# First layer's deformable sampling: tent arrays stored point by point, x tents and weight table in PSUM, table rows copied one by one for GpSimd

## Chip, cores and metric

One Trainium2 chip, one core. The metric is the device time of one execution in microseconds (us), median of the runs; each profile is of one execution. PE is TensorE, DVE VectorE, ACT ScalarE, POOL GpSimd, SP SyncE.

## What is computed

Two layers, each a sampling convolution and a mixture of experts, on x of shape (4, 16, 16, 64). Only the first layer's convolution is touched. Per position it has 8 groups of 8 channels and 9 sampling points with an offset (x and y) and a softmax mask:

```python
xp = x @ in_w + in_b
x1 = silu(batchnorm(depthwise3x3(x)))
offset = x1 @ off_w + off_b                       # 8 groups * 9 points * 2
mask = softmax((x1 @ mask_w + mask_b).reshape(N, H, W, 8, 9), -1)
# each point: bilinear sample of xp (zero outside) at its own place + offset
out = (samples * mask).sum(-1) @ out_w + out_b
x = x + out
```

A bilinear sample is a sum over image positions with weights max(0, 1 - |dx|) * max(0, 1 - |dy|), the product of two "tents".

## The kernel before

1024 positions lie as 128 partitions x J = 8 positions. The kernel is written engine by engine; each engine's instructions run in the order written, and semaphores join them. For offsets below 2 in size a point reaches 5 x 5 displacements around its own place (D0 = 5), and with the 3 x 3 points all lie in a window of N0 x N0 = 7 x 7 displacements; the four corners are left out, and so are those of the 5 x 5. If an offset is larger, a flag sends the program through a general loop, which does not run here.

**Tents.** `ox`, `oy` (offsets) and `ml` (mask logits) have 576 = 8 positions x 8 groups x 9 points columns, the point innermost. ACT makes tents as `Abs` (L618) and `Relu(1 - a)` (L620), in the order x tent 0, y tents 2 to 4, x tents 1 to 4. DVE makes y tents 0 and 1 (L1118 to L1121) and multiplies the other y tents by the mask's exponentials (L1127). Before that it adds biases (L1105), takes the maximum over the points (L1111) and subtracts it (L1112).

**Table.** 21 products of an x tent and a y tent (`tent_product`, L291) of 576 columns are summed into a table of 7 x 7 displacements x 64 columns, in `big` from `AW`. `A_OWNER` shares them out: POOL 10 and DVE 3 go through `ring` to PE, which adds them into banks 0 to 6 of PSUM by 3 matmuls with the identity (L757, 192 columns read with a step of 9); DVE keeps 8 and adds them to the table in SBUF (L1147). When a row of the table (one x displacement) is complete, DVE joins the bank to the SBUF part (`join`, L1139), 7 times. POOL first sets the table to zero (L451).

**Products.** For each of 45 displacements the slab of the image (`big`, loaded by SP's DMAs L365 into 7 shifted slabs, semaphore `slab0`) is multiplied by its table column, spread over 8 channels (`slab_product`, L298, 512 columns). `PATTERN` gives POOL 25, DVE 6 for PE, and DVE 14 that it sums itself (L1217). PE sums the other 31 in bank 7 (L770). Between these DVE computes the flag (L1190 to L1199, PE transposes it at L775, DVE ends it at L1065 and L1066 and loads it to a register), then the sums of the exponentials and their reciprocals (L1224, L1225). L1228 adds the two sums, L1290 multiplies by the reciprocals, and everything after waits for that.

In the second layer's sampling L269 is the like product (POOL from SBUF; DVE with weights in PSUM), L1487 DVE's sum with the running sum in PSUM, L277 makes those weights (two inputs in SBUF), L909 is PE's sum, L927 a matmul of 144 columns.

Of the kernel before, what the change touches and what calls it, by code (L numbers as in the profile page):

```python
# [30 lines left out]
ALU = mybir.AluOpType  # L31
# [4 lines left out]
P = 128  # L36
# [37 lines left out]
def program(nc, a, out):  # L74
    ctx = ExitStack()
    with ctx:
# [152 lines left out]
        TX, TY = N0 * SLAB0, N0 * SLAB0 + D0 * J * GP0  # L229
        AW = TY + D0 * J * GP0  # L230
        A_PITCH = N0 * J * G0
        NA = N0 * A_PITCH
        assert AW + NA <= BIG
# [61 lines left out]
        def slab_product(eng, w, slot):  # L295

            wx, wy = divmod(w, N0)
            return eng.tensor_tensor(V(ring, 0, slot, [[1, P], [C0, J * G0], [1, C0]]),  # L298
                                     bigv(wy * SLAB0 + wx * C, [C0, J * G0], [1, C0]),
                                     bigv(AW + wx * A_PITCH + wy * J * G0, [1, J * G0], [0, C0]), ALU.mult)  # L300

# [114 lines left out]
        def _(pool):  # L416
# [34 lines left out]
            gp.memset(bigv(AW, [1, NA]), 0.0).then_inc(sem("A_zero"), 1)  # L451

            i = 0
            for dx in range(D0):
                for dy in range(D0):
                    if A_OWNER(dx, dy) == "pool":
                        pool.wait_ge(sem("tenty"), dy + 1)
                        pool.wait_ge(sem("tentx"), dx + 1)
                        if i >= 3:  # L460
                            pool.wait_ge(sem("a_ps"), A_COUNT("pool", i - 3))
                        tent_product(gp, dx, dy, POOL0 + J * GP0 * (i % 3)).then_inc(sem("a_pool"), 1)
                        i += 1

            pool.wait_ge(sem("slab0"), 128)
            pool.wait_ge(sem("a_ps"), A_TOTAL)
            order = [w for w in DISPLACED if OWNER(w) == "pool"]
            for i, w in enumerate(order):
                pool.wait_ge(sem("A_done"), w // N0 + 1)
                if i >= 4:  # L470
                    pool.wait_ge(sem("acc0"), PE_COUNT(order[i - 4]))
                slab_product(gp, w, POOL0 + 512 * (i % 4)).then_inc(sem("pool_pr0"), 1)
# [107 lines left out]
        def _(act):  # L580
# [27 lines left out]
            made = {"tentx": 0, "tenty_raw": 0}  # L608
            for n, (name, src, base, k) in enumerate(
                    [("tentx", ox, TX, 0)] + [("tenty_raw", oy, TY, k) for k in range(DVE_TENTS, D0)] +  # L610
                    [("tentx", ox, TX, k) for k in range(1, D0)]):
                if n == 1:
                    act.wait_ge(sem("mask_in"), 1)
                    sc.activation(ml[:, :], ml[:, :], ACT.Exp).then_inc(sem("mask_e"), 1)
                    act.wait_ge(sem("offy"), 1)
                if n:
                    act.wait_ge(sem(before), made[before])
                sc.activation(abx[:, :], src[:, :], ACT.Abs, bias=cval[:, k:k + 1]).then_inc(sem("abx"), 1)  # L618
                act.wait_ge(sem("abx"), n + 1)
                sc.activation(bigv(base + k * J * GP0, [1, J * GP0]), abx[:, :], ACT.Relu, bias=1.0,  # L620
                              scale=-1.0).then_inc(sem(name), 1)
                made[name] += 1
                before = name

            act.wait_ge(sem(before), made[before])
            sc.activation(abx[:, :], ox[:, :], ACT.Abs).then_inc(sem("off_abs"), 1)
            act.wait_ge(sem("tenty"), DVE_TENTS)
# [66 lines left out]
        def _(pe):  # L694
# [56 lines left out]
            for n, (dx, dy) in enumerate(A_ORDER):  # L751
                who = A_OWNER(dx, dy)
                i = A_ORDER_OF(who).index((dx, dy))
                pe.wait_ge(sem("a_pool" if who == "pool" else "a_dve"), i + 1)
                slot = POOL0 + J * GP0 * (i % 3) if who == "pool" else J * GP0 * (i % 2)
# [6 lines left out]
            seen = {"pool": 0, "dve": 0}  # L762
            first = True
            for w in PE_ORDER:
                who = OWNER(w)
                i = seen[who]
                seen[who] += 1
                pe.wait_ge(sem("pool_pr0" if who == "pool" else "dve_pr0"), i + 1)
                slot = (POOL0 if who == "pool" else 0) + 512 * (i % 4)
                mm(bank(7, 0, P, [1, 512]), ident[:, :], ring[:, slot:slot + 512], start=first,  # L770
                   stop=(w == PE_ORDER[-1])).then_inc(sem("acc0"), 1)
                first = False
                if w == PE_ORDER[FLAG_AT[1]]:
# [1030 lines left out]
```

## Time and profile before

| | |
|---|---|
| median of 3 runs | 337.71 us (337.0 to 338.55) |
| profiled execution, its own time | 335.97 us |
| its span, first to last instruction | 334.2 us |
| mean granted clock of TensorE | 0.856 of full speed |
| busy share PE, DVE, ACT, POOL | 69%, 67%, 17%, 50% |
| DMA | 10.84 MB |

### The profile page before, as it was taken

Reading aid. Unit: us, or ns where it says so; the run is one execution under the profiler, and the core shown is the slowest. Engines: PE = TensorE matmul, PEld = TensorE weight load, DVE = VectorE, ACT = ScalarE, POOL = GpSimd, SP = SyncE. Lnnn points to the kernel's source line nnn. Section 1 sums busy time; section 2 is a strip of 40 time slices with the busy share of each in tenths; the row PEclk is TensorE's granted clock in tenths of the full one; section 3 lists DMA queues with packets and bytes.
Section 4 is the critical chain, followed back from the end, with each engine's and each line's share of the span. In section 5 each row is a group of like instructions: output and inputs, shape, how many; then the busy total and the mean of one; then the engine's idle time right before and its main releaser. Section 6 shows DMA issues by size and latency. Waiting matters only on the chain.

```text
span 334.2 us, 2821 instructions
## 1 busy us (share of the span) xinstructions
PE 230.9 (69%) x864; PEld 133.2 (40%) x864; DVE 223.2 (67%) x469; ACT 55.4 (17%) x91; POOL 168.7 (50%) x198
## 2 busy tenths in 40 slices
PE   1939595987948496998898477589689884038600
PEld 0715464632313264322353133257367744017500
DVE  7768999979998865747330876998995245502207
ACT  1306910000000014542401100011001203003100
POOL 5700762379849832681100599799975020530071
PEclk9989696978969959799999697999979996558955
DMA  4477920000000000000019100000000000010101
GB/s 150 134 148 153 204 48 0 0 0 1 0 0 1 1 2 0 1 0 3 0 31 206 30 3 0 1 0 0 3 0 0 2 0 0 17 55 0 41 20 43
DMA packets 8237, 10.84 MB, mean 32 GB/s; under 512 B 4571, under 2 KB 5083, under 8 KB 8155
## 3 DMA queue, kind: packets, MB, share of 16 engines
q1 hardware_dynamic: 7708, 10.12, 13.1%
q0 software_dynamic: 512, 0.53, 0.6%
q8 instruction: 7, 0.11, 0.1%
q14 instruction: 10, 0.08, 0.1%
HBM read 8.03 MB, written 2.61 MB: 32 GB/s over the span
## 4 chain that ended last, share of the span: by engine, by line
DVE 31%; PE 29%; issue 17%; POOL 8%; ACT 2%; DMA 1%; DVEq 0%; POOLq 0%; ACTq 0%
DVE ring L298 5%; PE ps L757 4%; PE ps L909 4%; DVE ps L1487 4%; DVE ring L1217 4%; POOL ring L269 3%; PE ps L884 3%; DVE ps L277 2%; POOL slots_in L568 2%; PE ps L935 2%; PE ps L797 2%; PE ps L720 2%; PE ps L819 2%; DVE ring L291 2%; PE ps L701 1%
## 5 line engine op out<-in xcount | busy, mean ns | idle before, releaser
L269 POOL TENSOR_TENSOR ring<-big 128x384 f32<-128x384 f32 x72 | 57.9, 842 | 5.0 <-DVE ps L1487 4.6
L909 PE MATMUL ps<-ring,ident 128*128 128x384 f32 x100 | 38.5, 528 | 12.5 <-POOL ring L269 6.3
L298 POOL TENSOR_TENSOR ring<-big 128x512 f32<-128x512 f32 x25 | 35.0, 1432 | 13.2 <-PE ps L770 6.7
L770 PE MATMUL ps<-ring,ident 128*128 128x512 f32 x62 | 33.6, 700 | 7.2 <-DVE ring L298 6.0
L701 PE MATMUL ps<-zero,ident 128*128 128x512 f32 x38 | 25.0, 813 | 16.8 <-DMA slots_in<-xn,idx_in 15.2
L757 PE MATMUL ps<-ring,ident 128*128 128x192 f32 x78 | 27.9, 529 | 7.8 <-DVE ring L291 4.3
L1487 DVE TENSOR_TENSOR ps<-ps,ring 128x384 f32<-128x384 f32 x46 | 25.8, 562 | 10.5 <-PE ps L909 8.4
L291 POOL TENSOR_TENSOR ring<-big 128x576 f32<-128x576 f32 x10 | 17.3, 1734 | 30.5 <-DVE big L1121 19.9
L909 PEld LDWEIGHTS ps<-ring,ident 128*128 128x128 f32 x100 | 18.9, 201 | 28.1 <-DVE ring L269 9.0
L438 POOL TENSOR_TENSOR rstd<-veps,mhalf 128x4 f32<-128x4 f32 x8 | 8.3, 1042 | 39.6 <-DVE veps L1044 39.5
L757 PEld LDWEIGHTS ps<-ring,ident 128*128 128x128 f32 x78 | 19.4, 253 | 16.4 <-DVE ring L291 5.5
L770 PEld LDWEIGHTS ps<-ring,ident 128*128 128x128 f32 x62 | 13.2, 222 | 26.9 <-issue 11.7
L298 DVE TENSOR_TENSOR ring<-big 128x512 f32<-128x512 f32 x20 | 22.5, 1154 | 1.2 <-DVE flagi L1066 1.0
L588 ACT COPY xT<-ps 64x512 f32<-64x512 f32 x8 | 4.5, 578 | 100.2 <-PE ps L709 100.2
L701 PEld LDWEIGHTS ps<-zero,ident 128*128 128x128 f32 x38 | 9.5, 267 | 27.1 <-DMA slots_in<-xn,idx_in 15.3
L269 DVE TENSOR_TENSOR ring<-big,ps 128x384 f32<-128x384 f32 x36 | 19.5, 546 | 0.1
L574 POOL DMA_INDIRECT big<-slots_out,idx_out x8 | 7.6, 952 | 23.5 <-DMA slots_out<-big 21.4
L1217 DVE TENSOR_TENSOR ring<-ring 128x512 f32<-128x512 f32 x13 | 15.1, 1165 | 0.1
L1369 DVE TENSOR_TENSOR big<-big,ps 128x512 f32<-128x512 f32 x16 | 10.3, 684 | 6.7 <-PE ps L805 6.7
L1147 DVE TENSOR_TENSOR big<-big,ring 128x576 f32<-128x576 f32 x8 | 14.3, 1790 | 0.2
L568 POOL DMA_INDIRECT slots_in<-xn,idx_in x8 | 8.0, 997 | 12.7 <-DVE idx_out L1544 10.6
L666 ACT COPY big<-ps 128x512 f32<-128x512 f32 x8 | 4.6, 586 | 58.4 <-PE ps L917 58.4
(269 smaller groups left out, 399.7 us busy)
## 6 DMA issues: line engine op xcount, KB each, us to landing
big<-pad SPq DMA_DIRECT2D x8, 392.0 KB, 9.0
big<-pad SPq DMA_DIRECT2D x8, 240.0 KB, 5.4
w<-in_w_dram SPq DMA_DIRECT2D x1, 520.0 KB
w<-in_w_dram SPq DMA_DIRECT2D x2, 256.0 KB
w<-in_w_dram SPq DMA_DIRECT2D x1, 512.0 KB
pad<-img SPq DMA_DIRECT2D x8, 64.0 KB, 2.0
pad<-zero SPq DMA_DIRECT2D x1, 484.0 KB, 3.7
pad<-zero SPq DMA_DIRECT2D x1, 400.0 KB, 4.3
```

Of the source, the lines that this page charges most:

```text
L269: return eng.tensor_tensor(V(ring, 0, slot * SP, [[1, P], [NJ * C, 3], [C1, NJ * G1], [1, C1]]), bigv((py + dy) * SLAB1 + (dx + j0) * C, [ ...
L291: return eng.tensor_tensor(ring[:, slot:slot + J * GP0], bigv(TY + dy * J * GP0, [1, J * GP0]), bigv(TX + dx * J * GP0, [1, J * GP0]), ALU ...
L298: return eng.tensor_tensor(V(ring, 0, slot, [[1, P], [C0, J * G0], [1, C0]]), bigv(wy * SLAB0 + wx * C, [C0, J * G0], [1, C0]), bigv(AW + ...
L568: gp.indirect_dma_start(out=slots_in.ap(), out_offset=bass.IndirectOffsetOnAxis(ap=idx_in[:, j:j + 1], axis=0), in_=xn[:, j, 0, :], in_off ...
L701: mm(bank(free_bank, 0, P, [1, 512]), ident[:, :], zero[:, 0:512], start=True, stop=True)
L757: last = mm(bank(px + dx, 0, P, [1, 3 * J * G0], off=dy * J * G0), ident[:, :], V(ring, 0, slot + 3 * px, [[1, P], [1, 3], [K, J * G0]]), ...
L770: mm(bank(7, 0, P, [1, 512]), ident[:, :], ring[:, slot:slot + 512], start=first, stop=(w == PE_ORDER[-1])).then_inc(sem("acc0"), 1)
L909: mm(bank(1 + i % 2, 0, P, [1, SP]), ident[:, :], ring[:, slot * SP:slot * SP + SP], start=(n == 0), stop=(n == len(srcs) - 1)).then_inc(s ...
L1147: v.tensor_tensor(dst, dst, V(ring, 0, SUM0 + J * GP0 * (i % 2), [[1, P], [3, 3], [1, 3], [K, J * G0]]), ALU.add).then_inc(sem("a_added"), 1)
L1217: v.tensor_tensor(acc, acc, V(ring, 0, OWN0 + 512 * ((i - 2) % 2), [[1, P], [1, 512]]), ALU.add).then_inc(sem("own_sum"), 1)
L1369: v.tensor_tensor(hid, hid, bank(6 + u % 2, 0, F0, [1, 512]), ALU.mult).then_inc(sem("hw"), 1)
L1487: v.tensor_tensor(acc, acc, ring[:, slot * SP:slot * SP + SP], ALU.add).then_inc(sem("s_add"), 1)
```

## The change

The three arrays hold the points outermost: column = point x 64 + position and group. The weights and biases are reordered outside to suit, and DVE's bias adds, maximum, subtraction and reduction get step 64. A tent product's three rows of points are then contiguous in `ring`, and PE reads them without a step.

Each x tent is written by ACT to PSUM bank 7 for its first 512 columns and to `big` (`TX8`) for the last 64; ACT waits with it until DVE has made all products of the x tent before. All 21 tent products are DVE's, as two instructions: 512 columns with the x tent from PSUM, 64 with both tents from SBUF (`A_SLOTS` = 3 slots). All are summed by PE; the table in SBUF, its zeroing, L1147 and the joins go. ACT copies rows 0 to 4 of the table to `big`, each as it is complete (`row_copied`); POOL has all 33 products of these rows (`POOL_W`), into 8 slots of its own in `big`. DVE has the 12 of rows 5 and 6 (`DVE_W`), with the table from PSUM. POOL's products are summed by DVE with the running sum in PSUM bank 0 (25 sums, `pool_sum`; 11 of them between the tent products of dx 2 to 4), except 7 that PE sums with DVE's 12.

```diff
         def tent_product(eng, dx, dy, slot):
-            return eng.tensor_tensor(ring[:, slot:slot + J * GP0],
-                                     bigv(TY + dy * J * GP0, [1, J * GP0]), bigv(TX + dx * J * GP0, [1, J * GP0]),
-                                     ALU.mult)
+            tent = TY + dy * J * GP0
+            eng.tensor_tensor(ring[:, slot:slot + 512], bigv(tent, [1, 512]), bank(7, 0, P, [1, 512]), ALU.mult
+                              ).then_inc(sem("a_dve"), 1)
+            eng.tensor_tensor(ring[:, slot + 512:slot + J * GP0], bigv(tent + 512, [1, J * G0]),
+                              bigv(TX8 + dx * J * G0, [1, J * G0]), ALU.mult).then_inc(sem("a_dve"), 1)
 ...
+            if w in POOL_W:
+                table = bigv(AW + wx * A_PITCH + wy * J * G0, [1, J * G0], [0, C0])
+            else:
+                table = bank(wx, 0, P, [1, J * G0], [0, C0], off=wy * J * G0)
 ...
 POOL:
-            gp.memset(bigv(AW, [1, NA]), 0.0).then_inc(sem("A_zero"), 1)
 ...
+            for i, w in enumerate(POOL_W):
+                pool.wait_ge(sem("row_copied"), w // N0 + 1)
+                if i >= PR_SLOTS:
+                    signal, count = POOL_FREED(i - PR_SLOTS)
+                    pool.wait_ge(sem(signal), count)
+                slab_product(gp, w, pool_slot(i, [C0, J * G0], [1, C0])).then_inc(sem("pool_pr0"), 1)
 ...
 ACT:
+            for k in range(1, D0):
+                distance(ox, k)
+                tent_x(k)
+                act.wait_ge(sem("tentx"), 2 * k + 2)
+                act.wait_ge(sem("a_ps"), A_BY(k - 1))
+                sc.copy(bigv(AW + (k - 1) * A_PITCH, [1, A_PITCH]), bank(k - 1, 0, P, [1, A_PITCH])
+                        ).then_inc(sem("row_copied"), 1)
 ...
 PE:
-                              V(ring, 0, slot + 3 * px, [[1, P], [1, 3], [K, J * G0]]), start=False,
+                              ring[:, slot + 3 * px * J * G0:slot + 3 * (px + 1) * J * G0], start=False,
 ...
+                if n == FLAG_AT[1]:
                     pe.wait_ge(sem("off_max"), 1)
+                    pe.wait_ge(sem("row_copied"), 3)
 ...
 DVE:
+            for q, (dx, dy) in enumerate(A_ORDER):
+                dve.wait_ge(sem("tentx"), 2 * dx + 2)
+                if q >= A_SLOTS:
+                    dve.wait_ge(sem("a_ps"), q - A_SLOTS + 1)
+                tent_product(v, dx, dy, J * GP0 * (q % A_SLOTS))
+                if dx >= 2 and dy >= 1:
+                    pool_sum()
 ...
+            for q, w in enumerate(DVE_W):
+                if q >= 4:
+                    dve.wait_ge(sem("acc0"), PE_SUMS.index(("dve", q - 4)) + 1)
+                slab_product(v, w, V(ring, 0, 512 * (q % 4), [[1, P], [C0, J * G0], [1, C0]])).then_inc(sem("dve_pr0"), 1)
 ...
+                pool_sum()
```

On DVE, in the table's second half, stood (L291 tent product, L1147 sum into the table, L1139 join):

```order
L291 TENSOR_TENSOR ring<-big 128x576 x2
L1139 TENSOR_TENSOR big<-big,ps 128x448
L1147 TENSOR_TENSOR big<-big,ring 128x3x192 x2
L291 TENSOR_TENSOR ring<-big 128x576 x2
L1139 TENSOR_TENSOR big<-big,ps 128x448
L1147 TENSOR_TENSOR big<-big,ring 128x3x192
L1139 TENSOR_TENSOR big<-big,ps 128x448 x3
```

Now it reads there (L293 and L295 are the two parts of a tent product, L1153 is the sum of a POOL product, `ps` its running sum or the x tent):

```order
L293 TENSOR_TENSOR ring<-big,ps 128x512
L295 TENSOR_TENSOR ring<-big 128x64
L1153 TENSOR_TENSOR ps<-big 128x512
L293 TENSOR_TENSOR ring<-big,ps 128x512
L295 TENSOR_TENSOR ring<-big 128x64
L1153 TENSOR_TENSOR ps<-ps,big 128x512
L293 TENSOR_TENSOR ring<-big,ps 128x512
```

Joins and sums into the table are gone from DVE, and sums of POOL's products, which stood behind the table, stand between the tent products.

On POOL, between the constants and the casts for the next stage, stood the table's zeroing, ten tent products and 25 slab products:

```order
L451 MEMSET big 128x3136
L291 TENSOR_TENSOR ring<-big 128x576 [waits tentx,tenty] x3
L291 TENSOR_TENSOR ring<-big 128x576 [waits a_ps,tentx,tenty] x7
L298 TENSOR_TENSOR ring<-big 128x512 [waits A_done,a_ps,slab0]
L298 TENSOR_TENSOR ring<-big 128x512 [waits A_done] x3
L298 TENSOR_TENSOR ring<-big 128x512 [waits acc0,A_done] x21
```

and now 33 slab products alone (L305):

```order
L305 TENSOR_TENSOR big<-big 128x512 [waits row_copied,slab0]
L305 TENSOR_TENSOR big<-big 128x512 [waits row_copied] x7
L305 TENSOR_TENSOR big<-big 128x512 [waits v_sum,row_copied] x14
L305 TENSOR_TENSOR big<-big 128x512 [waits acc0,row_copied]
L305 TENSOR_TENSOR big<-big 128x512 [waits v_sum,row_copied] x2
```

The wait for the whole table (`a_ps`) has given way to one for a row's copy, and from the ninth product on POOL waits for DVE's sums (`v_sum`) or PE's (`acc0`).

## Rows read from the trace of the kernel before

**Rows 1.** Windows: us, busy us of each engine, PEclk, DMA share, GB/s

```profile
36.80:70.60 33.80, 28.23 (x79) 19.55 (x80) 31.08 (x28) 6.36 (x10) 16.84 (x11) 0.80 0.22 42
70.60:115.50 44.90, 33.50 (x63) 13.01 (x61) 43.37 (x44) 0.00 (x0) 37.89 (x32) 0.85 0.00 0
```

**Rows 2.** Chain of waits from 66 to 116 us, shares by line

```profile
by line: DVE ring L298 32.0%; DVE ring L1217 25.2%; issue 18.4%; PE ps L770 7.6%; PE ps L757 6.2%; DVE big L1139 2.4%; DVEq L1203 1.6%; DVE ring L1228 1.4%; DVE m L1224 1.3%; DVE flagf L1197 1.3%; DVE r L1225 1.1%; DVE flagf L1198 0.5%; DVE
```

**Rows 3.** Timeline of DVE: start, us, instructions, idle before and releaser

```profile
68.91 1.68 DVE L1139 TENSOR_TENSOR big<-big,ps 128x448 f32<-128x448 f32 x3 [2.38 <-PE ps L757]
...
113.37 0.75 DVE L1224 TENSOR_REDUCE m<-ml 128x64 f32<-128x576 f32 x1
...
114.74 0.69 DVE L1228 TENSOR_TENSOR ring<-ring,ps 128x512 f32<-128x512 f32 x1
```

**Rows 4.** Instructions of line 298: ns min/median/max, first and last start

```profile
L298 POOL TENSOR_TENSOR ring<-big x25: 1069/1517/1585, 69.0 to 109.1; 128x512 f32<-128x512 f32 x25
L298 DVE TENSOR_TENSOR ring<-big x20: 679/1272/1558, 70.6 to 111.2; 128x512 f32<-128x512 f32 x20
```

**Rows 5.** Timeline, POOL alone, POOL beside DVE, DVE alone

```profile
69.01 2.11 POOL L298 TENSOR_TENSOR ring<-big 128x512 f32<-128x512 f32 x2 [6.50 <-issue]
...
71.07 11.88 POOL L298 TENSOR_TENSOR ring<-big 128x512 f32<-128x512 f32 x8
...
95.41 1.28 DVE L298 TENSOR_TENSOR ring<-big 128x512 f32<-128x512 f32 x2
```

**Rows 6.** Instructions of line 269, second layer

```profile
L269 POOL TENSOR_TENSOR ring<-big x72: 831/837/980, 192.7 to 254.6; 128x384 f32<-128x384 f32 x72
L269 DVE TENSOR_TENSOR ring<-big,ps x36: 543/546/555, 193.9 to 255.4; 128x384 f32<-128x384 f32 x36
```

**Rows 7.** Timeline of DVE and ACT before the first tent product

```profile
29.21 0.76 DVE L1112 TENSOR_TENSOR ml<-ml,m 128x576 f32<-128x576 f32 x1
...
30.93 0.68 ACT L614 ACTIVATE ml<-ml 128x576 f32<-128x576 f32 x1
...
34.58 3.34 DVE L1127 TENSOR_TENSOR big<-big,ml 128x576 f32<-128x576 f32 x3
...
35.35 0.68 ACT L620 ACTIVATE big<-abx 128x576 f32<-128x576 f32 x1
```

**Rows 8.** Instructions of line 1147

```profile
L1147 DVE TENSOR_TENSOR big<-big,ring x8: 1168/1974/2329, 41.8 to 65.3; 128x576 f32<-128x576 f32 x8
```

**Rows 9.** Timeline of PE, runs of passes

```profile
44.20 6.37 PE L757 MATMUL ps<-ring,ident 128*128 128x192 f32 x18
...
96.75 4.56 PE L770 MATMUL ps<-ring,ident 128*128 128x512 f32 x5 [0.83 <-DVE ring L298]
...
102.43 4.88 PE L770 MATMUL ps<-ring,ident 128*128 128x512 f32 x11
...
219.01 1.15 PE L927 MATMUL ps<-w_ua,big 128*128 128x144 f32 x8
```

**Rows 10.** Windows for clock and slabs; timeline of PE at its longest pause

```profile
42.00:43.00 1.00, 1.00 (x4) 0.90 (x4) 1.00 (x1) 0.97 (x3) 1.00 (x1) 0.50 1.04 201
43.00:44.00 1.00, 1.00 (x4) 0.69 (x4) 1.00 (x1) 0.42 (x1) 0.07 (x1) 0.96 0.83 156
...
95.54 0.37 PE L775 MATMUL ps<-ident,flagf 128*1 128x128 f32 x1 [3.41 <-DVE flagf L1199]
```

**Rows 11.** Timeline of POOL and DVE around the one-column instructions

```profile
92.92 2.55 POOL L298 TENSOR_TENSOR ring<-big 128x512 f32<-128x512 f32 x2
...
94.49 1.00 DVE L1199 SCALAR_TENSOR_TENSOR flagf<-flagf 128x1 f32<-128x1 f32 x1
```

**Rows 12.** Timeline of DVE after the flag's last step

```profile
104.09 1.19 DVE L298 TENSOR_TENSOR ring<-big 128x512 f32<-128x512 f32 x1 [0.95 <-DVE flagi L1066]
```

**Rows 13.** Instructions of line 277, and one of them in the timeline

```profile
L277 DVE TENSOR_TENSOR ps<-big x4: 641/1904/4409, 193.2 to 238.4; 128x216 f32<-128x216 f32 x4
...
208.45 3.05 DVE L277 TENSOR_TENSOR ps<-big 128x216 f32<-128x216 f32 x1
```

More of the change, by code:

```diff
@@ L607, in _ @@
             act.wait_ge(sem("cval"), 1)
[L608 to L617, printed above, removed]
-                sc.activation(abx[:, :], src[:, :], ACT.Abs, bias=cval[:, k:k + 1]).then_inc(sem("abx"), 1)
[L619 to L623, printed above, removed]
@@ L625, in _, with distance, tent_x @@
-            act.wait_ge(sem(before), made[before])
+            n_abs = 0
+            def distance(src, k):
+                nonlocal n_abs
+                sc.activation(abx[:, :], src[:, :], ACT.Abs, bias=cval[:, k:k + 1]).then_inc(sem("abx"), 1)
+                n_abs += 1
+                act.wait_ge(sem("abx"), n_abs)
+            def tent_x(k):
+                if k:
+                    act.wait_ge(sem("a_dve"), 2 * A_BY(k - 1))
+                sc.activation(bank(7, 0, P, [1, 512]), abx[:, 0:512], ACT.Relu, bias=1.0, scale=-1.0
+                              ).then_inc(sem("tentx"), 1)
+                sc.activation(bigv(TX8 + k * J * G0, [1, J * G0]), abx[:, 512:J * GP0], ACT.Relu, bias=1.0, scale=-1.0
+                              ).then_inc(sem("tentx"), 1)
@@ new lines, in _ @@
+            distance(ox, 0)
+            act.wait_ge(sem("offy"), 1)
+            tent_x(0)
+            act.wait_ge(sem("mask_in"), 1)
+            sc.activation(ml[:, :], ml[:, :], ACT.Exp).then_inc(sem("mask_e"), 1)
+            act.wait_ge(sem("tentx"), 2)
+            for k in range(DVE_TENTS, D0):
+                distance(oy, k)
+                sc.activation(bigv(TY + k * J * GP0, [1, J * GP0]), abx[:, :], ACT.Relu, bias=1.0, scale=-1.0
+                              ).then_inc(sem("tenty_raw"), 1)
+                act.wait_ge(sem("tenty_raw"), k - DVE_TENTS + 1)
@@ L627, in _ @@
+            for k in range(D0 - 1, POOL_ROWS):
+                sc.copy(bigv(AW + k * A_PITCH, [1, A_PITCH]), bank(k, 0, P, [1, A_PITCH])).then_inc(sem("row_copied"), 1)
             act.wait_ge(sem("tenty"), DVE_TENTS)
@@ L1172, in _ @@
-            for wx in range(D0 - 1, N0):
-                join(wx)
-            dve.wait_ge(sem("A_done"), N0)
-            dve.wait_ge(sem("slab0"), 128)
-            order = [w for w in DISPLACED if OWNER(w) == "dve"]
-            own = [w for w in DISPLACED if OWNER(w) == "sum"]
-            acc = V(ring, 0, SUM0, [[1, P], [1, 512]])
-            def product(w, slot):
-                return slab_product(v, w, slot)
-            todo = list(order)
-            k = 0
-            for i in range(len(own) + 1):
-                if i == FLAG_AT[0]:
+            acc = V(ring, 0, SUM0, [[1, P], [1, 512]])
@@ new lines, in _, with pool_sum @@
+            n_sum = 0
+            def pool_sum():
+                nonlocal n_sum
+                if n_sum == 0:
+                    dve.wait_ge(sem("row_copied"), 1)
+                else:
+                    dve.wait_ge(sem("v_sum"), n_sum)
+                i = DVE_SUMS[n_sum + 1]
+                dve.wait_ge(sem("pool_pr0"), i + 1)
+                first = pool_slot(DVE_SUMS[0], [1, 512]) if n_sum == 0 else bank(0, 0, P, [1, 512])
+                dst = bank(0, 0, P, [1, 512]) if n_sum < len(DVE_SUMS) - 2 else acc
+                v.tensor_tensor(dst, first, pool_slot(i, [1, 512]), ALU.add).then_inc(sem("v_sum"), 1)
+                n_sum += 1
```

201 lines of the change are left out of this document (65 added, 136 removed).

## The prediction

> **What bounds the kernel now.** I read the stages first. The first layer's sampling has two parts: the table of weights (36.8 to 70.6 us) and the 45 products with it (70.6 to 115.5). DVE is busy for 31.08 of 33.8 us and 43.37 of 44.9; PE and POOL have room [rows 1]. The chain of waits says the same of 66 to 116 us: DVE's products (L298) 32% and its sums (L1217) 25.2%, and only then PE [rows 2]. DVE stops twice for PE (2.38 us before the last joins, once for the flag), so a step taken off DVE moves the end. The end that counts is L1228, which adds DVE's sum to PE's: it starts at 114.74 and takes 0.69 us, so 115.4 [rows 3].
>
> **Why DVE is so slow there.** With both inputs in SBUF a DVE instruction and a POOL product stretch each other. L298 takes 679 ns at best and 1272 in the median on DVE, 1069 and 1517 on POOL [rows 4]. Eight POOL products beside such DVE work take 11.88 us, one each (11.88 - 1.52) / 7 = 1.48 us; two alone take 2.11, so 1.03 each [rows 5]. DVE alone issues one every 0.60 us (1.28 us for two [rows 5]), beside POOL every 1.48. With one input in PSUM it doesn't happen: in the second layer POOL's L269 has 831 to 980 ns while DVE's L269, with the weights in PSUM, stays at 543 to 555 [rows 6]. That is the change's lever: it puts x tents, table and sum in PSUM.
>
> **Start.** DVE's third L1127 waits for ACT's relu, which ends at 36.03, and the second was stretched by POOL's first tent product; three took 3.34 us [rows 7]. POOL's ten tent products go, so DVE starts tents at about 36.1 + 0.75 = 36.9 instead of 38.0. The strided edits (bias adds, L1111, L1112 and their new forms) cost nothing up to 0.95 us: the softmax shift ends at 29.97, the exponential waits for its table load until 30.93 [rows 7]. The strided max may go from 0.74 to 1.2 us (strided L1147 takes 1168 ns at least [rows 8], plain L1112 760 [rows 7]); that stays under the cover.
>
> **Table, tents of dx 0 and 1.** Eight tent products are now all DVE's, each 0.60 us plus a 64-column one. For the latter: 679 ns for 512 columns [rows 4] and 546 for 384 [rows 6] make 1.04 ns a column and 0.15 us fixed, so 0.21 for 64, less the 0.08 by which instructions overlap: 0.15 (bounds 0.07, its columns alone, and 0.30). 8 x 0.75 = 6.0. Bank 7 holds one x tent, so ACT may write the next only when DVE has read the last: a relu of 512 and one of 64 stand on the path, estimated from L620's 0.68 for 576 [rows 7] at 1.05 us with hand-overs (0.7 to 1.5). Twice: 2.1. The first eight end at 45.0. PE: its strided 192-column passes come every (6.37 - 0.52) / 17 = 0.344 us with the clock at full [rows 9]. Contiguous passes follow the columns: 0.429 us for 512 (11 take 4.88), 0.123 for 144, 0.85 for 512 at 1.2 GHz [rows 9]. So 192 cost 0.161 or 0.32, a tent's six passes 0.97 or 1.92 us instead of 2.06. The clock was at 0.50 at 42 us [rows 10], early in the table's build, before which PE has nothing to do; that pause stays, so with three slots PE holds DVE back by some 1.5 us. POOL's first product waits for the slabs, whose packets end at 43.8 [rows 10]; I take 44.8, when row 0 has long been copied.
>
> **Table, dx 2 to 4, beside POOL.** 13 tents, 11 of them followed by one sum of a POOL product. DVE's own pitch would be 0.60 + 0.15 + 0.60 = 1.35. But the 64-column product still has both inputs in SBUF. L1199, one column wide, took 1.00 us because POOL was in a product: both end at 95.5 [rows 11]. POOL's period is 1.03, so a round of 1.35 tends to last two periods, 2.06, except where POOL itself waits for a slot: I take 1.85. 11 x 1.85 + 2 x 1.0 + two hand-overs 2.1 = 24.5. The table ends at 45.0 + 1.5 + 24.5 = 71, no sooner than now. What is gained is that 19 products and 11 sums are done by then. The seven joins and eight L1147 (1168 to 2329 ns each) are gone [rows 8].
>
> **After the table.** 12 products and 14 sums at 0.60: 15.6 us. Flag: three reduces 0.75, the min (0.76, or 1.62 beside POOL), two tiny ones: 3.8; the sum of the exponentials and its reciprocal, 1.37 from 113.37 to 114.74, 1.7 in the strided form; the last flag step 1.4, of it 0.95 idle before the next product; waits and L1228 1.0 [rows 3, 12]. Together 23.5. PE has 19 sums of 0.86, 16 us, hidden at 2.4 GHz; at 1.2 they are 32 and bound. The three reduces leave PE without input for over 3 us; before, PE's 3.41 us pause for the flag [rows 10] was followed by passes of 0.85 us, the lower level [rows 9]. So I add 2.5 for PE. End: 71 + 23.5 + 2.5 = **97**, against 115.4: **18 us** less. POOL's 33 products need 33 x 1.03 = 34 us from 44.8; with eight slots they follow DVE's sums and end some 5 us before it. ACT's five copies of 448 columns, one instruction each like L620, hide under DVE; so do the waits added ahead of PE's flag transpose. The 334.2 - 115.5 = 218.7 us behind it are untouched. The profiled execution took 335.97 us (span 334.2); less 18 is 318. The median of the runs is 337.71, 1.7 above it, so **319.7 us** in such runs. A change of 0.5% (1.7 us) is about what can be told from none.
>
> **The port, row against rule.** L277 on DVE, 216 columns with both inputs in SBUF, took 641, 757 (by the median), 3051 and 4409 ns [rows 13]: at 0.8 us per L269 that is three and five POOL products of waiting in two of four. L298 on DVE never took more than 1558 ns, one POOL product and itself [rows 4]. The Trainium skill (SBUF — State Buffer, Who interferes with whom) says that whichever of the two starts first holds the shared port for its whole instruction and the other fully blocks until it finishes. By that each small product waits for at most one of POOL's, which gives the sum above; rows 11 agree, the long L277 don't, and they make the first rival.
>
> **Rivals.**
> 1. *POOL gets in again and again.* Each of the some 18 small products beside POOL waits one more product, some 0.6 to 1.0 us. POOL can't run on for long: it needs a slot that only DVE's sums free. The table ends 10 us later, the end is at 107: gain 8.5, 329 us. Two of four L277 speak for it, L298 against. Chance 0.22.
> 2. *POOL's slot waits leave the port free.* The rounds take 1.35 to 1.45: some 6 us less, end 91, gain 24.5: 313 us. Chance 0.07.
> 3. *PE stays at 1.2 GHz.* 63 x 2 x 0.32 = 40 us of table passes from 37.7, then 19 x 1.71 = 32, with gaps: 113. Gain 2.5, 335 us. Before, the clock was at 0.80 and 0.85 of full in these stages [rows 1]. Chance 0.05.
> 4. *Slower.* The same small product (L295 of the changed kernel), at the mean of the four L277, 2.2 us, in spite of the slots: 18 x (2.2 - 0.5) = 31 us more, end 128, 350 us. It turns slower where the mean wait is over 0.5 + 18 / 18 = 1.5 us. Chance 0.03.
>
> The forecast has 0.63. Range 312.5 to 329: case 1 is at its upper end and case 2 at its lower, cases 3 and 4 are left out. Faster by over 0.5%: 0.63 + 0.22 + 0.07 and half of case 3, 0.94; within 0.5% 0.03; slower 0.03.
>
> **What would show it.** Right: in the table stage the DVE product with a PSUM input stays at 0.68 us and POOL's at 1.07; the 64-column ones have a median between 0.3 and 0.9 us; the last table pass of PE ends near 71; POOL starts its first product at 44 to 45 and its last near 92; the final add is at 96 to 98. Wrong: 64-column products of 2 us and more, PE idle for ACT's relu by more than 1.5 us at each dx, PE passes of 192 columns that stay at 0.344, or a stage behind 97 us that is longer than 218.7.

## The result, and the profile after it

The changed kernel takes **315.35 us** (median of 4 runs, 315.16 to 315.57) against 337.36 (4 runs, 336.58 to 338.55): ratio 0.9345, 95% interval 0.9315 to 0.9375, 22.0 us less. The forecast was 319.7 with a range of 312.5 to 329. The profiled execution took 315.29 us, its span is 313.6, the mean clock 0.857. Between the two profiled executions the difference is 20.7 us (335.97 - 315.29): the kernel before was profiled in one of its faster executions.

Windows of the changed kernel (columns as in [rows 1]): from the first tents to the slabs' arrival, the rest of the table, the products behind it, and everything after.

```profile
33.50:44.00 10.50, 9.56 (x43) 9.56 (x44) 6.43 (x17) 2.80 (x7) 0.00 (x0) 0.70 1.03 202
44.00:70.50 26.50, 17.91 (x85) 14.49 (x83) 23.08 (x37) 5.08 (x10) 20.85 (x20) 0.94 0.00 1
70.50:94.60 24.10, 19.68 (x39) 7.27 (x39) 21.72 (x37) 1.12 (x2) 17.24 (x24) 0.93 0.01 2
94.60:313.60 219.00, 150.92 (x645) 88.38 (x645) 121.74 (x331) 35.22 (x64) 100.95 (x131) 0.83 0.07 17
```

The table ends where it did (70.5 against 70.6). But 20 of POOL's products lie in its second part, and the stage behind it takes 24.1 us instead of 44.9 [rows 1]. Behind it, 219.05 us against 218.8 (334.2 - 115.4) have not moved.

The instructions of the new lines (ns min/median/max, first and last start): L293 and L295 are the 512 and the 64 columns of a tent product, L305 a product with a table column, L1153 a sum of a POOL product.

```profile
L293 DVE TENSOR_TENSOR ring<-big,ps x21: 669/680/690, 33.6 to 67.8; 128x512 f32<-128x512 f32 x21
L295 DVE TENSOR_TENSOR ring<-big x21: 218/403/951, 34.2 to 68.4; 128x64 f32<-128x64 f32 x21
L305 POOL TENSOR_TENSOR big<-big x33: 1071/1077/1521, 45.5 to 88.8; 128x512 f32<-128x512 f32 x33
L305 DVE TENSOR_TENSOR ring<-big,ps x12: 677/678/687, 70.6 to 90.2; 128x512 f32<-128x512 f32 x12
L1153 DVE TENSOR_TENSOR ps<-ps,big x23: 685/693/700, 50.1 to 91.5; 128x512 f32<-128x512 f32 x23
L1153 DVE TENSOR_TENSOR ps<-big x1: 1482/1482/1482, 47.7 to 47.7; 128x512 f32<-128x512 f32 x1
```

What has one operand in PSUM stays within 3% of its median beside POOL. What has both in SBUF doesn't: 64 columns take 218 to 951 ns, and the one sum that starts from two SBUF inputs 1482 instead of 693. POOL's products are back from 1517 ns [rows 4] to 1077.

Timeline of the changed kernel, start of the sampling and the first rounds beside POOL (columns as in [rows 3]; L1098 is the first tap of the depthwise convolution, L752 the matmuls for offsets and mask):

```profile
12.46 0.52 DVE L1098 TENSOR_SCALAR cm<-cm,w_dc 128x572 f32<-128x572 f32 x1
...
21.14 3.20 PE L752 MATMUL ps<-w_om,o_tok 64*64 64x216 f32 x32 [3.25 <-ACT o_tok L596]
...
33.56 0.69 DVE L293 TENSOR_TENSOR ring<-big,ps 128x512 f32<-128x512 f32 x1
...
45.48 4.62 POOL L305 TENSOR_TENSOR big<-big 128x512 f32<-128x512 f32 x4 [33.22 <-DMA big<-pad]
...
47.70 1.48 DVE L1153 TENSOR_TENSOR ps<-big 128x512 f32<-128x512 f32 x1 [2.14 <-POOL big L305]
...
51.31 0.95 DVE L295 TENSOR_TENSOR ring<-big 128x64 f32<-128x64 f32 x1
52.18 0.69 DVE L1153 TENSOR_TENSOR ps<-ps,big 128x512 f32<-128x512 f32 x1
52.78 0.67 DVE L293 TENSOR_TENSOR ring<-big,ps 128x512 f32<-128x512 f32 x1
53.37 0.95 DVE L295 TENSOR_TENSOR ring<-big 128x64 f32<-128x64 f32 x1
```

The last rows are one round: from one L295 to the next 2.06 us, two of POOL's periods. Later POOL has to wait for a free slot in each round, and a round takes 1.91 us (POOL's product, the L295 that waits for it, and the next L295):

```profile
66.14 1.08 POOL L305 TENSOR_TENSOR big<-big 128x512 f32<-128x512 f32 x1 [0.83 <-DVE ps L1153]
66.50 0.79 DVE L295 TENSOR_TENSOR ring<-big 128x64 f32<-128x64 f32 x1
...
68.41 0.79 DVE L295 TENSOR_TENSOR ring<-big 128x64 f32<-128x64 f32 x1
```

Two of the rows above are not what the forecast had: the first tent starts at 33.56, not 36.9, and DVE stands for 2.14 us before its first sum.

### The profile page after: what moved, and what is told of

It is laid out like the page before. It is cut to its first block, busy times and chain, and to the rows that moved or that the text cites. A ratio compares the mean times of both kernels' runs of the same rounds, so it can differ in the third digit from the quotient of the medians.

```text
span 313.6 us, 2914 instructions
## 1 busy us (share of the span) xinstructions
PE 217.3 (69%) x888; PEld 132.1 (42%) x888; DVE 199.6 (64%) x489; ACT 58.1 (19%) x101; POOL 147.2 (47%) x195
## 4 chain that ended last, share of the span: by engine, by line
PE 27%; DVE 27%; POOL 17%; issue 14%; DMA 7%; SPq 5%; ACT 2%; POOLq 0%; DVEq 0%; ACTq 0%
POOL ring L270 8%; PE ps L917 6%; DMA big<-pad 4%; PE ps L892 3%; SPq L314 3%; DVE ps L278 3%; DVE ps L1153 3%; DVE ring L295 2%; POOL slots_in L562 2%; PE ps L943 2%; POOL rstd L446 2%; PE ps L716 2%; PE ps L827 2%; POOL big L305 2%; PE ps L735 2%
## 5 line engine op out<-in xcount | busy, mean ns | idle before, releaser
L305 POOL TENSOR_TENSOR big<-big 128x512 f32<-128x512 f32 x33 | 35.0, 1091 | 42.7 <-DMA big<-pad 33.2
L917 PE MATMUL ps<-ring,ident 128*128 128x384 f32 x100 | 40.2, 543 | 12.8 <-POOL ring L270 7.0
L716 PE MATMUL ps<-zero,ident 128*128 128x512 f32 x38 | 26.4, 850 | 16.8 <-DMA slots_in<-xn,idx_in 15.2
L917 PEld LDWEIGHTS ps<-ring,ident 128*128 128x128 f32 x100 | 19.6, 209 | 29.7 <-issue 10.8
L770 PEld LDWEIGHTS ps<-ring,ident 128*128 128x128 f32 x126 | 24.1, 220 | 17.1 <-DVE ring L295 16.9
L293 DVE TENSOR_TENSOR ring<-big,ps 128x512 f32<-128x512 f32 x21 | 14.3, 679 | 4.7 <-PE ps L770 3.1
L1153 DVE TENSOR_TENSOR ps<-ps,big 128x512 f32<-128x512 f32 x23 | 15.9, 691 | 1.1 <-POOL big L305 1.0
L778 PE MATMUL ps<-ring,ident 128*128 128x512 f32 x24 | 13.9, 685 | 3.6 <-DVE ring L305 3.4
L724 PE MATMUL ps<-ident,xn 128*128 128x128 f32 (+1 forms) x32 | 5.7, 315 | 10.2 <-DVE xn L1056 10.2
L805 PE MATMUL ps<-big,w 64*128 64x512 f32 x32 | 10.5, 730 | 1.4 <-ACT big L651 1.4
L651 ACT ACTIVATE big<-ps,b 128x512 f32<-128x512 f32 x16 | 10.0, 687 | 7.5 <-PE ps L805 7.4
```

The lines of the kernel that those rows point to most:

```text
L293: eng.tensor_tensor(ring[:, slot:slot + 512], bigv(tent, [1, 512]), bank(7, 0, P, [1, 512]), ALU.mult).then_inc(sem("a_dve"), 1)
L305: return eng.tensor_tensor(dst, bigv(wy * SLAB0 + wx * C, [C0, J * G0], [1, C0]), table, ALU.mult)
L716: mm(bank(free_bank, 0, P, [1, 512]), ident[:, :], zero[:, 0:512], start=True, stop=True)
L778: mm(bank(7, 0, P, [1, 512]), ident[:, :], product, start=(n == 0), stop=(n == len(PE_SUMS) - 1)).then_inc(sem("acc0"), 1)
L805: mm(bank(2 * (k % 2) + n, 0, F0, [1, 512]), w_10[C * n:C * n + C, F0 * i:F0 * i + F0], V(big, C * n, XT2 + 512 * hf, [[1, C], [1, 512]]), ...
L917: mm(bank(1 + i % 2, 0, P, [1, SP]), ident[:, :], ring[:, slot * SP:slot * SP + SP], start=(n == 0), stop=(n == len(srcs) - 1)).then_inc(s ...
```

## The experiments

Eleven kernels. Four ask where the start's 3.3 us and the slabs' wait come from, four what each part of the change is worth, three what TensorE's clock costs. The kernel before ran beside each group; its medians there were 337.4 to 338.2, so differences of less than 0.8 us between groups are not read as one.

### The zeroing of the table

In the kernel before, POOL's zeroing of the table (L451) and the first tap of the depthwise convolution on DVE (L1090) lie side by side:

```profile
12.06 2.71 POOL L451 MEMSET big<- 128x3136 f32 x1
12.35 2.74 DVE L1090 TENSOR_SCALAR cm<-cm,w_dc 128x572 f32<-128x572 f32 x1
```

Without the zeroing the same instruction (L1098 above) takes 0.52 us. To tell whether that is the cause, the zeroing was put back into the changed kernel (on columns that nothing reads yet):

```diff
+            gp.memset(bigv(PR, [1, 3136]), 0.0).then_inc(sem("A_zero"), 1)
+            pool.wait_ge(sem("A_zero"), 1)
```

> The changed kernel with a memset of 3136 columns put back on POOL where the table's zeroing stood (into POOL's own slots). Theory A, zeroing and DVE's first tap exclude each other, and the slabs hide it now: L1098 goes from 0.52 to 2.7 us and the first tent starts 2.2 to 3.4 us later, but the first sum still waits for POOL's second product at 47.7, so the end moves by 0 to 1 us (315.3 to 316.4). Rival B, the earlier start is itself what was gained: the whole 2.2 to 3.4 us come back (317.5 to 318.8). Rival C, the start moved for another reason: L1098 stays at 0.52.

Measured: 318.08 us (317.81 to 318.57), ratio 0.9434 (0.9382 to 0.9485), 2.7 more than the change. Theory A's 0 to 1 us was wrong, and rival B's range holds the time. The tap is back to its old length:

```profile
12.05 2.71 POOL L459 MEMSET big<- 128x3136 f32 x1
12.34 2.74 DVE L1100 TENSOR_SCALAR cm<-cm,w_dc 128x572 f32<-128x572 f32 x1
```

The first tent starts at 38.29 instead of 33.56. The tap gives 2.2 us of it; nearly all of the rest comes from the offsets' matmuls, which now begin at 23.23 instead of 21.14 and take 5.83 us instead of 3.20:

```profile
23.23 5.83 PE L754 MATMUL ps<-w_om,o_tok 64*64 64x216 f32 x32 [5.79 <-ACT o_tok L598]
```

The clock was granted at 0.75 of full from 24 to 33.5, against 0.97 in the changed kernel. Of the 4.7 us, 2.0 don't reach the end. POOL starts at 45.33, as in the change, but DVE comes to its first sum only at 50.54 instead of 47.70, and stands for no product of POOL before it; so it is DVE's own work, and no longer the slabs, that sets the pace there. The other way round, in the kernel before alone, POOL waits with the zeroing for the end of the convolution:

```diff
+            pool.wait_ge(sem("dwc"), 1)
```

> The kernel before with the table's zeroing behind the depthwise convolution, where POOL is idle. Theory A: the first tap (L1090) falls from 2.74 to 0.5 us and all of it counts, since nothing there waits for the slabs: 2.2 to 3.4 us less than before (334 to 335.2). Rival C: no difference (337.4).

Measured: 334.07 us (332.78 to 335.25, 10 runs), ratio 0.9903 (0.9874 to 0.9932): 3.3 us less for one wait, in theory A's range, and the first tent at 34.52 instead of 38.01. So some 3 of the change's 22 us are nothing of its design, but a collision that it happened to remove.

The Trainium skill (SBUF — State Buffer, Who interferes with whom) says that a DVE `tensor_scalar` may run in a mode that uses the port pair shared with GpSimd, and that the one that issues first keeps it for its whole instruction. These rows agree: the tap ends 0.3 us behind the zeroing's end at 14.77. No row names the tap's mode; alone it takes 0.52 us for 572 columns, less than the 0.68 us of 512 columns with two inputs.

### The small products joined

The 64-column product stood in each round with both inputs in SBUF. Here the five of one x tent are one instruction of 320 columns (ten slots in `ring` instead of three):

```diff
-            eng.tensor_tensor(ring[:, slot + 512:slot + J * GP0], bigv(tent + 512, [1, J * G0]),
-                              bigv(TX8 + dx * J * G0, [1, J * G0]), ALU.mult).then_inc(sem("a_dve"), 1)
+            eng.tensor_tensor(V(ring, 0, J * GP0 * TENT_SLOT(dx, 0) + 512, [[1, P], [J * GP0, D0], [1, J * G0]]),
+                              bigv(TY + 512, [J * GP0, D0], [1, J * G0]),
+                              bigv(TX8 + dx * J * G0, [0, D0], [1, J * G0]), ALU.mult).then_inc(sem("a_tail"), 1)
```

> The changed kernel with the 64-column products of one x tent made by one instruction of 320 columns (5 instead of 21 with two inputs in SBUF; ten slots for tents). Theory A, DVE's rounds last two POOL products only because of the small product's wait: rounds fall from about 1.95 us to 1.2 to 1.35, the table ends 4 to 7 us earlier, total 309 to 311.5. Rival B, POOL's slots and ACT's hand-over of bank 7 set the pace: less than 1.5 us gained (over 313.8).

Measured: 308.66 us (307.94 to 310.6), ratio 0.917 (0.9112 to 0.9227), 6.7 less than the change. The rounds beside POOL, DVE's timeline:

```profile
50.01 0.67 DVE L293 TENSOR_TENSOR ring<-big,ps 128x512 f32<-128x512 f32 x1
50.60 0.69 DVE L1158 TENSOR_TENSOR ps<-ps,big 128x512 f32<-128x512 f32 x1
51.20 0.67 DVE L293 TENSOR_TENSOR ring<-big,ps 128x512 f32<-128x512 f32 x1
51.80 0.69 DVE L1158 TENSOR_TENSOR ps<-ps,big 128x512 f32<-128x512 f32 x1
```

A round is 1.19 us instead of 2.06. Theory A is right, and its range (309 to 311.5) was 0.3 us too cautious: the smallest instruction set the pace, by the POOL product it waited for. The edit also frees DVE from PE, by the ten slots (in the change DVE stood 3.1 us for PE, all of it before 43). That is not where the gain lies: the first sum starts at 47.41, only 0.3 us sooner than in the change, since it waits for the slabs, and the table's last pass ends at 64.0 instead of 70.5.

### The slabs first

SP issued 17 loads of weights ahead of the image's store and the slab loads. Here the store and the slab loads are issued first; the lines are the same.

> The changed kernel with the image's store and the slabs' loads issued on SP ahead of the weight loads (from w_10 on). Theory A, POOL's start at 45.5 waits for the slabs: they land by about 35 us, POOL starts when row 0 is copied, at about 41, and DVE's idle 2.1 us before the first sum goes: 2 to 4.5 us less (311 to 313.4). Rival B, an earlier POOL only meets DVE's small products and its slots earlier: less than 1 us (over 314.3).

Measured: 313.93 us (312.39 to 314.29, 5 runs), ratio 0.9312 (0.9262 to 0.9362), 1.4 less. POOL's first product starts at 39.62 instead of 45.48; DVE then meets POOL in more of its small products. That lies between both theories. DVE's 2.14 us before its first sum go; that part of them comes back at the port is argued from the rows. The profiled execution was the fastest of the five (312.39). With the joined small products as well:

> The changed kernel with both earlier edits: the 64-column tent products joined to one of 320 columns per x tent (which alone gave 6.7 us), and SyncE's queue with the image store and the slab loads ahead of the weight loads (which alone gave 1.4 us by medians and 3.0 in the profiled execution). Theory A (the two are separate waits, one on GpSimd's products, one on the slabs): both add up, 305.5 to 307.5 us, GpSimd's first product near 40, the sampled first layer done (o_tok) by 88. Rival B (with the joined products the sums at the end are bound by GpSimd's 33 products or by VectorE's own work, so an earlier GpSimd brings nothing): within 0.5 us of 308.7.

Measured: 307.46 us (307.25 to 307.6), ratio 0.9102 (0.9074 to 0.9131): 1.2 less than the joined products alone, so the two do add. POOL began at 42.40, later than expected: it no longer waits for the slabs but for the first table row's copy.

```profile
POOL big L309 <- ACT big L640: 30.2, 1, 30.2
```

(Waits of POOL in that kernel: us in total, times, longest.)

### Which of the PSUM operands pays

First the x tents. They go back to SBUF, and each tent product is one instruction again; table columns and running sum stay in PSUM.

```diff
-            eng.tensor_tensor(ring[:, slot:slot + 512], bigv(tent, [1, 512]), bank(7, 0, P, [1, 512]), ALU.mult
-                              ).then_inc(sem("a_dve"), 1)
...
+            eng.tensor_tensor(ring[:, slot:slot + J * GP0], bigv(tent, [1, J * GP0]),
+                              bigv(TX8 + dx * J * GP0, [1, J * GP0]), ALU.mult).then_inc(sem("a_dve"), 1)
```

> The changed kernel with the x tents in SBUF instead of PSUM's bank 7: each tent product is one instruction of 576 columns with two SBUF inputs. The running sum and VectorE's table columns stay in PSUM. Theory A (the 64-column product has two SBUF inputs already and waits for GpSimd's product in each round, so one wait per round is paid in either case): the round grows only by what the one product lasts once it has the port, from about 1.9 to 2.1 us, in 13 rounds 0 to 3 us, and four hand-overs of bank 7 go: 314 to 318 us. Rival B (the x tents in PSUM are what makes the overlap possible): with the long product shut out and shutting out GpSimd, the rounds are 2.8 us or more and GpSimd ends late, 322 to 328 us.

Measured: 313.46 us (313.25 to 313.95), ratio 0.928 (0.925 to 0.9311): 1.9 **less** than the change, 0.5 below theory A's range and far from rival B's. The one instruction, line 293 of this kernel:

```profile
L293 DVE TENSOR_TENSOR ring<-big x21: 749/1021/1629, 34.7 to 65.8; 128x576 f32<-128x576 f32 x21
```

Its median of 1021 ns is less than the two medians that it replaces, 680 + 403. The rounds beside POOL:

```profile
51.83 1.02 DVE L293 TENSOR_TENSOR ring<-big 128x576 f32<-128x576 f32 x1
52.77 0.69 DVE L1147 TENSOR_TENSOR ps<-ps,big 128x512 f32<-128x512 f32 x1
53.37 1.02 DVE L293 TENSOR_TENSOR ring<-big 128x576 f32<-128x576 f32 x1
```

That is 1.54 us a round instead of 2.06. POOL's products beside these rounds:

```profile
50.65 12.43 POOL L303 TENSOR_TENSOR big<-big 128x512 f32<-128x512 f32 x8
```

POOL makes one product in each such round (1.55 us each), and two in the change's round of 2.06 (1.03 each). So in both kernels DVE waits once per round for POOL. In the split form DVE's sum and its 512 columns, 1.2 us, lie between two waits, longer than POOL's 1.03, so that POOL has begun a second product; here only the sum does, 0.6 us. The x tents in PSUM cost some 2 us as built. With the small products joined (308.66 us, 1.19 us a round) they are worth 4.8 us against this kernel.

Then the running sum, in SBUF instead of bank 0:

```diff
-                first = pool_slot(DVE_SUMS[0], [1, 512]) if n_sum == 0 else bank(0, 0, P, [1, 512])
-                dst = bank(0, 0, P, [1, 512]) if n_sum < len(DVE_SUMS) - 2 else acc
+                first = pool_slot(DVE_SUMS[0], [1, 512]) if n_sum == 0 else V(ring, 0, OWN0, [[1, P], [1, 512]])
+                dst = V(ring, 0, OWN0, [[1, P], [1, 512]]) if n_sum < len(DVE_SUMS) - 2 else acc
```

> The changed kernel with the running sum of the sampled products in SBUF instead of PSUM's bank 0, so that each of VectorE's 25 sums has two SBUF inputs and an SBUF output. Theory A (a sum with two SBUF inputs waits for GpSimd's product at hand, as the 64-column product does, and blocks the next): each sum takes 1.1 to 1.5 us instead of 0.69, and GpSimd's products start later by as much; 25 sums give 10 to 20 us: 325 to 335 us. Rival B (one SBUF wait per round is there anyway, and behind the table VectorE has slack): under 4 us more, 315 to 319 us.

Measured: 321.5 us (321.31 to 322.0), ratio 0.9521 (0.949 to 0.9552), 6.2 more than the change. A round beside POOL is now 2.51 us, with two waits in it (L295 0.27 us over its 0.22 alone, L1153 0.89 over 0.69):

```profile
52.27 0.68 DVE L293 TENSOR_TENSOR ring<-big,ps 128x512 f32<-128x512 f32 x1
52.86 0.49 DVE L295 TENSOR_TENSOR ring<-big 128x64 f32<-128x64 f32 x1
53.28 1.58 DVE L1153 TENSOR_TENSOR ring<-ring,big 128x512 f32<-128x512 f32 x1
54.78 0.68 DVE L293 TENSOR_TENSOR ring<-big,ps 128x512 f32<-128x512 f32 x1
```

The mechanism is theory A's; the size is between the two, because the sums' median is 960 ns and not 1.1 to 1.5 us: from 64.7 to 78.7 us, where POOL waits for a slot in each round, seven sums in a row take 0.68 to 0.69 us. The running sum in PSUM is worth about 6 us.

Last, the overlap itself. POOL waits for the last copied row, DVE makes no sum between tents, and PE adds POOL's products last:

```diff
-                pool.wait_ge(sem("row_copied"), w // N0 + 1)
+                pool.wait_ge(sem("row_copied"), POOL_ROWS)
...
-                if dx >= 2 and dy >= 1:
-                    pool_sum()
```

> The changed kernel with nothing beside the table's build: GpSimd waits for all five of its copied table rows before its first product, VectorE makes no sum between tents, and TensorE adds GpSimd's late products behind VectorE's. The rest (x tents in PSUM, the running sum in PSUM, the table in PSUM) stays. Theory A (the overlap is the gain): the table is done by 56 to 59, then 33 products at 1.04 to 1.08 us end at 92 to 95 and the output is at 96 to 99: 317 to 320 us, 2 to 5 us slower than the change. Rival B (the rounds beside GpSimd cost as much as they hide: 13 rounds of 1.9 us against 0.95 alone): within 1 us of 315.35 or faster, since nothing then waits for the port.

Measured: 322.6 us (320.8 to 323.66), ratio 0.9559 (0.9525 to 0.9594), 7.2 more. The table is done a little before 57, as theory A had it, and POOL's 33 start at 57.32; they don't run through, but wait for DVE's sums (3.7 us in all), and DVE waits 2.47 us at the end for PE, which has POOL's products last:

```profile
57.32 20.21 POOL L305 TENSOR_TENSOR big<-big 128x512 f32<-128x512 f32 x18 [45.30 <-ACT big L641]
...
99.37 0.69 DVE L1189 TENSOR_TENSOR ring<-ring,ps 128x512 f32<-128x512 f32 x1 [2.47 <-PE ps L778]
```

So theory A in kind, though the time is 2.6 above its range; up to 1.5 us (2.47 against 0.94 in the change) are due to PE's other order. The overlap is worth 5 to 7 us of the 22. The same kernel without any overlap still beats the one before by 15 us. The larger part must come from what it keeps: the table without joins and sums in SBUF, products and sums on DVE that no longer meet POOL at the port, and the missing zeroing. Of these only the zeroing (some 3 us) and the running sum (6) were taken back by themselves; how the rest divides is not shown.

### The clock

TensorE's first table passes run at 1.2 GHz in the change: the mean from 33.5 to 44 is 0.70 of full. More filler work ahead of it:

```diff
-            keep_clock(4, 4)
+            keep_clock(7, 4)
...
+            for wx in range(5):
+                mm(bank(wx, 0, P, [1, A_PITCH]), ident[:, :], zero[:, 0:A_PITCH], start=True, stop=False,
+                   skip_group_check=True)
```

> The changed kernel with TensorE given more to do ahead of the table: seven instead of four filler products of 512 columns before the offsets' matmuls, and five of the seven matmuls that zero the table's PSUM banks a second time behind the seventh, so that TensorE works until about 34. The sums are the same. Theory A (the first tents from 33.5 run against TensorE at 1.2 GHz, and GpSimd's first product and the rounds come late by it): the granted clock between 33.5 and 44 rises from 0.70 to 0.9 or more, 2 to 3 us less, 312 to 313.5. Rival B (the slabs and the port set that stretch, whatever the clock): the clock rises and the time stays within 0.7 us of 315.35.

Measured: 316.11 us (315.24 to 316.49), ratio 0.9351 (0.9314 to 0.9388), no gain over the change's 0.9345 (by the medians 0.76 us more, a hair outside rival B's 0.7): rival B in kind. The clock did rise, and the tents did come sooner, but for nothing. The window from 33.5 to 44, and the two rows that took the gain back:

```profile
33.50:44.00 10.50, 9.63 (x57) 9.26 (x58) 7.71 (x20) 3.96 (x8) 0.00 (x0) 1.00 1.04 204
...
46.98 9.78 POOL L305 TENSOR_TENSOR big<-big 128x512 f32<-128x512 f32 x9 [34.81 <-DMA big<-pad]
49.19 1.48 DVE L1156 TENSOR_TENSOR ps<-big 128x512 f32<-128x512 f32 x1 [6.03 <-POOL big L305]
```

DVE stands for 6.03 us instead of 2.14 for POOL's second product, and POOL for the slabs, which in this execution, the slowest of the four, landed 1.5 us later. The other 2.4 us of this longer stand are what the tents had gained (the first of dx 2 starts at 41.61 instead of 44.01). With the slabs first and the joined products that cover is gone, so the same edit was tried there. First a new order alone: ACT makes the 64-column x tent before it waits for bank 7 and the next distance before it copies a row; DVE makes the joined product of the next x tent while ACT hands bank 7 over.

```diff
+                if q + 1 == A_BY(dx) and dx + 1 < D0:
+                    dve.wait_ge(sem("tentx"), 2 * dx + 3)
+                    if dx:
+                        dve.wait_ge(sem("a_ps"), A_BY(dx - 1))
+                    tent_tails(v, dx + 1)
```

> The kernel with joined 64-column products and the slab loads first (307.46 us), in another order: ScalarE makes the 64-column x tent before it waits for bank 7, and the next distance before it copies a table row; VectorE makes the joined 64-column product of the next x tent behind the last tent of this one, while ScalarE hands bank 7 over. Theory A (at each of the four hand-overs of bank 7 VectorE stands for 0.3 to 3.3 us in that kernel): 2 to 4 us less, 303.5 to 305.5. Rival B (TensorE at 1.2 GHz ends the first x tent's tents at 41.5 and GpSimd's 33 products end last anyway): within 0.7 us of 307.46.

Measured: 307.11 us (306.41 to 307.75), ratio 0.9099 (0.9065 to 0.9134): 0.35 less than 307.46, rival B. TensorE at half clock ends the first x tent so late that ACT copies the first row at 41.58, and DVE waits behind it. Then with the fillers on top:

> The two edits together: the order with the 64-column products ahead, and TensorE's fillers. Theory A (both terms are there and add): 301 to 303.5 us, the best of all kernels. Rival B (one of them is hidden by the other, or GpSimd's 33 products at 1.06 us from its first one at 39 to 40 end last): no better than the better of the two alone by 0.7 us.

Measured: **303.19 us** (303.12 to 304.72), ratio **0.8992** (0.8951 to 0.9032), 3.9 less than the order alone and 12.2 less than the change. The two kernels, clock window and the first row's copy, without the fillers:

```profile
33.50:44.00 10.50, 8.17 (x35) 8.17 (x36) 8.56 (x14) 4.72 (x9) 1.75 (x2) 0.67 0.92 183
...
41.58 0.53 ACT L642 COPY big<-ps 128x448 f32<-128x448 f32 x1 [3.16 <-PE ps L777]
```

and with them:

```profile
33.50:44.00 10.50, 9.38 (x58) 9.33 (x58) 10.04 (x17) 4.40 (x10) 5.37 (x5) 1.00 0.92 186
...
37.96 0.53 ACT L642 COPY big<-ps 128x448 f32<-128x448 f32 x1 [0.70 <-PE ps L780]
```

The first row is copied 3.6 us sooner, POOL starts at 38.63 instead of 42.25, and the layer's output is at 82.92 instead of 86.54. Of the 3.6 us, 1.2 lie ahead of the first tent product (33.53 instead of 34.69): the offsets' matmuls took 3.20 us instead of 4.51. The other 2.4 are the table's passes. In the pair above, the change and the change with fillers, the offsets' matmuls took 3.20 us in both, so there the fillers had only the 2.4 us to give, and POOL's wait for the slabs took them.

The same edit gave nothing in one kernel and 3.9 us in another. One difference is what POOL waits for behind it: the slabs' DMA in the first (34.81 us), the first row's copy in the second (26.39 us). The others are the joined products, the new order, and the offsets' matmuls just named; no run has the fillers with the early slabs alone, so the account by the slabs is argued from the waits.

## Why the prediction was right, and where it was off

| step | forecast | measured |
|---|---|---|
| first tent | 36.9 | 33.56 |
| from it to the first tent of dx 2 | 9.6 us | 10.45 us |
| from there to the table's end | 24.5 us | 26.5 us |
| from there to the end of the final add | 26.0 us | 24.05 us |
| that end | 97 | 94.55 |
| behind it | 218.7 us | 219.05 us |

The direction and mechanism held: 22 us less by DVE's time, in the forecast's own case and not in a rival's. That the end came within 2.5 us of the forecast is in part luck: it had the start 3.3 us too late and the stage behind the table 1.95 too long, but the table 2.85 too short. Its own signs were met but for four, narrowly: POOL's first product started at 45.48 and not by 45, its last at 88.8 and not near 92, the final add at 93.86 and not at 96 to 98, and what follows took 0.35 us more than the 218.7 that it named as a limit. Of the difference of 4.35 us (319.7 - 315.35), 2.4 are these rows; some 2 are the 1.7 us that the forecast added for the median standing above the profiled execution, and rounding. For the changed kernel profiled run and median are 0.06 apart, so that addition was a guess about runs and not a part of the kernel.

**Start: the step that was off most.** "DVE starts tents at about 36.1 + 0.75 = 36.9 instead of 38.0" counted POOL's tent products that go, and left out that the zeroing goes too, although the change's list for POOL began with it. It cost DVE 2.2 us (2.74 against 0.52). Another 1.3 us are clock: the 32 matmuls of the offsets took 4.49 us before and take 3.20 now. The two kernels with the zeroing put back and moved show the sum, 2.7 and 3.3 us of the time. But that the clock's part comes from the zeroing, by the matmuls' later start, is not shown. In the kernel with joined products, which has no zeroing, they start as early as in the change and take 4.88 us:

```profile
21.03 4.88 PE L756 MATMUL ps<-w_om,o_tok 64*64 64x216 f32 x32 [3.48 <-ACT o_tok L600]
```

**Table, dx 0 and 1.** Short by 0.85 us: DVE waited 3.1 us for PE and not 1.5, since PE's clock stayed at the lower level until 39.5 (0.50 of full from 34 to there), while one of the two hand-overs overlapped with that wait. A tent took the 0.75 us that were estimated (33.56 to 34.30 is 0.74), and L295 alone 218 ns (0.21).

**Table beside POOL.** The period of 2.06 us was right (51.31 to 53.37), and so was the median of the small product, 0.40 us in the 0.3 to 0.9 named. The mean round of 1.85 us that the sum used was near too: 2.06 at first, 1.91 once POOL waits for slots. Missed was the first sum: it needs POOL's second product, 2.14 us of standing, and itself has two inputs in SBUF, 1.48 us. A wait that is added at the point where two engines first meet deserved a term.

**The rule on the port.** The rule of the Trainium skill cited in the forecast (SBUF — State Buffer, Who interferes with whom) gives at most one POOL product of waiting for each small one, and this trace agrees. The longest L295 took 951 ns, less than 218 + 1077, and in the round with the sum in SBUF (two such instructions) both were stretched by less than one product of POOL (0.27 and 0.89 us). Rival 1 and rival 4 are refuted for this place. The weights' product of the second layer (L277 before, L278 now), which fed them, still has waits of several products (381 to 4745 ns), and why was not tried.

**Rivals 2 and 3.** What rival 2 set out from came true, POOL waited for slots eight times, 9.5 us in all, five of them in the table's build, but the rounds there took 1.91 us and not 1.35 to 1.45: each DVE sum frees a slot, POOL begins at once, and the next L295 meets its product. Rival 3 is refuted by the clock, 0.94 and 0.93 of full in the two stages from 44 to 94.6.

**Behind the table.** 24.05 us against 23.5 without the clock term; the 2.5 us for PE's clock were not needed (0.93 of full in that window, against 0.85 in the kernel before [rows 1]). DVE waited for PE only 0.79 us at the table's end and 0.94 before the final add.

**Strided edits.** Free, as said: the strided maximum took 1.15 us, the shift behind it ended at 26.99, and ACT was loading its table until 27.6.

## To carry to other kernels

When a change drops an instruction, look at what runs beside it on the engine that shares its port, also when nothing waits for it: here a zeroing that nobody waited for cost some 3 us. Splitting an instruction to move its operands to PSUM paid here only when no piece with both operands in SBUF was left in the round, not even one of 64 columns. And a gain in front of a wait for a transfer can be lost in that wait: the clock fillers gave nothing where POOL waited for the slabs, and 3.9 us in a kernel where it didn't.

## What had not been expected of the hardware

- A GpSimd memset of 3136 columns, which reads nothing, held up a VectorE `tensor_scalar` of 572 columns (one tensor in SBUF and one column of weights): 2.74 us instead of 0.52, in both kernels whose rows are shown, where they met; it took 0.52 where the zeroing was gone or moved.
- Two SBUF operands in a 576-column product beside GpSimd took 1.02 us, in rounds of 1.54 us, where the 64-column product alone was stretched from 0.22 to 0.95 in rounds of 2.06. The wider product cost less than the split one. How the two engines fall into step is argued from the rows, and was not tried by itself.
- The offsets' 32 matmuls took 3.20, 4.5 to 4.9 or 5.83 us, by the clock that was granted. With four fillers ahead of them and no zeroing, three profiles have 3.20 (the change, slabs first, POOL behind the table) and five have 4.51 to 4.88 (joined products, both edits, x tents in SBUF, sum in SBUF, the new order), though the queue in front of them is the same on TensorE; both kernels with seven fillers have 3.20. Each is one execution, so whether the kernel or the execution decides is open. The first tent moves with it by 1.1 to 1.6 us (33.56 in the change, 35.14 with joined products).
